# Shared experts' 704 features in parts of 384 and 320, gate and up of the last 64 in one chunk

## What is computed

```python
xn = layernorm(x)
x = x + attention(xn, Wq, Wk, Wv, Wo) \
      + routed(xn, top2 of 8 experts, 352 features each) \
      + (silu(xn @ sg.T) * (xn @ su.T)) @ sd.T      # shared: sg, su [704, 512], sd [512, 704]
```

## Time and profile before

| | us |
|---|---|
| median of 3 timed runs | 1118.25 (1118.01 to 1118.48) |
| profiled execution | 1127.01 |
| its span, first to last instruction | 1125.0 |
| norm and project phases | 0 to 183 |
| attend phase | 183 to 757 |
| out phase and start of the routed one | 757 to 820 |
| routed phase | 820 to 1125 |
| mean granted TensorE clock | 0.969 |

### The profile page before, as it was taken

The page is one execution under the profiler, slowest core; times in us unless marked ns, Lnnn a source line. Parts: engine busy times, 40 slices in busy tenths (PEclk is TensorE's granted clock), DMA queues, the critical chain, the costliest instruction groups (busy, mean ns, idle before and its releaser), DMA issues. The chain is left out here.

```text
span 1125.0 us, 18890 instructions
## 1 busy us (share of the span) xinstructions
PE 1046.2 (93%) x5379; PEld 817.6 (73%) x5380; DVE 784.6 (70%) x1675; ACT 637.9 (57%) x1278; POOL 506.4 (45%) x568
## 2 busy tenths in 40 slices
PE   6999979888899998999999999998989999999994
PEld 4767867666677776777778777776867777778872
DVE  6732324565688887788888888865568888888872
ACT  3323211265588786787787887872155555565550
POOL 0013903388756564556566565651013443333321
PEclk9999989988899999999999999998989999999997
DMA  6989996255543553644445426118789444443432
GB/s 213 322 335 361 136 293 231 94 67 102 132 133 77 150 148 75 163 118 136 115 113 151 126 64 191 45 39 266 243 283 278 90 76 75 75 72 68 71 54 35
DMA packets 106201, 163.61 MB, mean 145 GB/s; under 512 B 53984, under 2 KB 64480, under 8 KB 102656
## 3 DMA queue, kind: packets, MB, share of 16 engines
q1 hardware_dynamic: 95776, 141.82, 44.1%
q0 software_dynamic: 9760, 20.49, 10.0%
q10 hardware_dynamic: 576, 0.26, 0.1%
HBM read 101.25 MB, written 61.28 MB: 144 GB/s over the span
## 5 line engine op out<-in xcount | busy, mean ns | idle before, releaser
L1198 POOL TENSOR_TENSOR prob_lo<-prob,prob_hi 128x512 fp32r<-128x512 f32 (+2 forms) x320 | 308.3, 977 | 203.3 <-ACT prob_hi L1243 147.0
L1236 ACT ACTIVATE prob<-ps_s 128x512 f32<-128x512 f32 (+3 forms) x384 | 188.0, 490 | 127.1 <-PE ps_s L1463 77.1
L1243 ACT ACTIVATE prob_hi<-prob 128x512 fp32r<-128x512 f32 (+3 forms) x384 | 198.6, 517 | 12.4 <-ACT row_stage L1217 12.4
L1862 DVE TENSOR_TENSOR rw_lo<-gu_sb,rw_hi 128x704 fp32r<-128x704 f32 x156 | 138.8, 893 | 52.7 <-ACT rw_hi L1806 47.7
L1306 DVE CUSTOM_DVE_ANT_0 ps_m<-ps_m,causal 128x384 f32<-128x384 f32 (+3 forms) x256 | 126.7, 495 | 69.2 <-PE ps_m L1432 66.9
L1806 ACT ACTIVATE rw_hi<-gu_sb 128x704 fp32r x156 | 123.5, 794 | 62.8 <-PE ps_ru L1895 43.6
L1458 PE MATMUL ps_s<-qs,ks 97*128 97x512 f32 (+3 forms) x384 | 140.4, 366 | 9.4 <-ACT prob L1236 9.2
L1779 POOL DMA_INDIRECT out<-work,slot_table x39 | 63.5, 1627 | 181.1 <-DVE work L1847 148.2
L1481 PE MATMUL ps_o<-prob_hi,vs 128*66 128x512 f32 (+3 forms) x384 | 133.1, 347 | 10.4 <-issue 9.6
L1432 PE MATMUL ps_m<-ks,qs 96*128 96x512 f32 (+3 forms) x384 | 139.1, 362 | 0.6 <-DVE maxima L1306 0.2
L1483 PE MATMUL ps_o<-prob_lo,vs 128*66 128x512 f32 (+3 forms) x384 | 132.0, 344 | 0.0
(11 more groups left out here) (201 smaller groups left out, 2353.0 us busy)
## 6 DMA issues: line engine op xcount, KB each, us to landing
xt<-xt_blocks SPq DMA_DIRECT2D x7, 2048.0 KB, 9.1
v_rows<-work SPq DMA_DIRECT2D x16, 512.0 KB, 3.0
xt_blocks<-xt SPq DMA_DIRECT2D x4, 2048.0 KB, 11.3
qk_hi<-work SPq DMA_DIRECT2D x8, 1024.0 KB, 4.7
qk_lo<-work SPq DMA_DIRECT2D x8, 1024.0 KB, 7.5
qs<-qk_hi SPq DMA_DIRECT2D x64, 128.0 KB, 2.9
ks<-qk_hi SPq DMA_DIRECT2D x64, 128.0 KB, 3.2
vs<-v_rows SPq DMA_DIRECT2D x32, 256.0 KB, 4.7
```

What stands on the lines that cost most here:

```text
L1198: nc.gpsimd.tensor_tensor(prob_lo[:, s % NPL, 0:w], prob[:, s % NP, 0:w], prob_hi[:, s % NPH, 0:w].bitcast(F32), ALU.subtract).then_inc(lo ...
L1236: nc.scalar.activation(prob[:, s % NP, 0:w], ps_s[s % NS][:, 0:w], ACT.Exp, scale=SCALE).then_inc(exp_done, 1)
L1243: nc.scalar.activation(prob_hi[:, s % NPH, 0:w], prob[:, s % NP, 0:w], ACT.Copy).then_inc(hi_ready, 1)
L1862: nc.vector.tensor_tensor(w_lo[:, k, :], chunk(e, k), w_hi[:, k, :].bitcast(F32), ALU.subtract).then_inc(w_lo_ready, 1)
```

## The change

The parts become 384 and 320 features: SHARED is three chunks of 128 for part 0, and 128, 128 and 64 for part 1. The last chunk of part 1 is mixed: its 64 gate and 64 up features are laid side by side in sg, one group of 12 matmuls computes both, gates in partitions 0 to 63 and ups in 64 to 127 of one bank. A unit of part 1 then has 96 matmuls instead of 108. Since the group count of these units is odd, BANK says which bank a unit begins with. Tanh, gate and hidden follow each other on the one bank; hidden and its two successors of a mixed chunk are put one step later. The first two y-adds are brought forward where the bank's next use would come in an earlier step. Gate, up and down weights of the shared experts are laid out over all 704 features in HBM, and part 0 is loaded in three DMAs instead of four. slot and pick now share the memory of started.

```diff
 FCH = [(0, 128), (128, 128), (256, 96)]
+FSH = NSH * F
+SHARED = [[(0, 128), (128, 128), (256, 128)], [(0, 128), (128, 128), (256, 64)]]
+PART_AT = [0, 3 * P]
+def is_mixed(part, k):
+    return SHARED[part][k][1] < P
...
-    UP_END = [2 * GROUP * (k + 1) for k in range(NF)]
-    PER_UNIT = UP_END[-1] + 4 * 3 * NF
+    GATE_END, UP_END = [], []
+    for part in range(2):
+        ends = [0]
+        for k in range(NF):
+            ends += [ends[-1] + GROUP, ends[-1] + (1 if is_mixed(part, k) else 2) * GROUP]
+        GATE_END.append(ends[1::2])
+        UP_END.append(ends[2::2])
+    PER_UNIT = [up_end[-1] + 4 * 3 * NF for up_end in UP_END]
+    BANK = [sum(is_mixed(n // NTB, NF - 1) for n in range(unit)) % 2 for unit in range(UNITS)]
...
-    TANH_AT, GATE_AT = chunks_at(GROUP, 1), chunks_at(GROUP, 2)
-    HIDDEN_AT, HIDDEN_HI_AT, HIDDEN_LO_AT = [chunks_at(2 * GROUP, lag) for lag in (1, 2, 3)]
+    TANH_AT, GATE_AT = [chunks_at(GATE_END, lag, lag) for lag in (1, 2)]
+    HIDDEN_AT, HIDDEN_HI_AT, HIDDEN_LO_AT = [chunks_at(UP_END, lag, lag + 1) for lag in (1, 2, 3)]
...
-        ADD_AT.setdefault(step_of(n // 4, Y_END[n % 4] - 1) + 1, []).append(n)
+        unit, q = divmod(n, 4)
+        end = Y_END[unit // NTB][q]
+        taken = step_of(unit, end + (3, 9)[q]) if q < 2 else ALL
+        ADD_AT.setdefault(min(step_of(unit, end - 1) + 1, taken), []).append(n)
...
-    SPLIT_AT = {step_of(LAST, UP_END[k] - 1) + 2: [k] for k in range(NF)}
+    SPLIT_AT = {step_of(LAST, UP_END[0][k] - 1) + 2: [k] for k in range(NF)}
...
+        def second_places(k, gates, ups):
+            f0, w = SHARED[1][k]
+            if is_mixed(1, k):
+                return (gates, slice(f0, f0 + w)), (gates, slice(f0 + w, f0 + 2 * w))
+            return (gates, slice(f0, f0 + w)), (ups, slice(f0, f0 + w))
...
-                    f0, w = FCH[k]
+                    f0, w = SHARED[1][k]
                     wait(sp, gu_lo_ready, 2 * k)
                     for n, src in enumerate((sgate, sup)):
-                        sp.dma_start(gu_raw[:, n, :, 0:w], src[1, :, :, f0:f0 + w]
+                        at = PART_AT[1] + f0
+                        sp.dma_start(gu_raw[:, n, :, 0:w], src[:, :, at:at + w]
...
+                        up_of = ps_f[bank][w:2 * w, :] if mixed(n) else ps_f[1 - bank][0:w, :]
+                        nc.vector.scalar_tensor_tensor(hid[0:w, :], gated[0:w, :], 0.5, up_of,
+                                                       ALU.mult, ALU.mult).then_inc(hid_ready, 1)
...
-                    last = nc.tensor.matmul(ps_f[part][0:w, :],
-                                            (w_hi, w_lo, w_hi)[term][:, kc, f0:f0 + w],
+                    last = nc.tensor.matmul(ps_f[(BANK[unit] + part) % 2][:, :],
+                                            (w_hi, w_lo, w_hi)[term][:, kc, f0:f0 + P],
...
-                        if q < 2:
-                            pe.wait_ge((gated_ready, hid_ready)[q], NF * (unit + 1))
+                        if q >= 2:
+                            pe.wait_ge(y_added, 4 * unit + q - 1)
+                        elif mixed(chunks - 1):
+                            pe.wait_ge(hid_ready, chunks - 1 + q)
                         else:
-                            pe.wait_ge(y_added, 4 * unit + q - 1)
+                            pe.wait_ge((gated_ready, hid_ready)[q], chunks)
...
-                pool.wait_ge(shared_loaded, 64)
-                w = FCH[-1][1]
-                for n, (raw, (hi, lo)) in enumerate(zip((sg_raw, su_raw), shared_w)):
+                pool.wait_ge(shared_loaded, 48)
+                for n, (raw, (hi, lo)) in enumerate(zip((sg_raw, su_raw, sd_raw), shared_w)):
```

More of the change, by code:

```diff
@@ L43 @@
 FCH = [(0, 128), (128, 128), (256, 96)]
+FSH = NSH * F
+SHARED = [[(0, 128), (128, 128), (256, 128)], [(0, 128), (128, 128), (256, 64)]]
+PART_AT = [0, 3 * P]
+assert PART_AT[1] + sum(w for _, w in SHARED[1]) == FSH
+def is_mixed(part, k):
+    return SHARED[part][k][1] < P
 NORM_SLOTS, YS = 4, 4
@@ L843, in step_cost, with chunks_at @@
         return cost
-    FILL = fill_counts([step_cost(s) for s in range(ALL)], UNITS * PER_UNIT, 0, STEPS + AHEAD, 228.0)
+    FILL = fill_counts([step_cost(s) for s in range(ALL)], BEGIN[-1], 0, STEPS + AHEAD, 228.0)
     FILLED = [sum(FILL[:s]) for s in range(ALL + 1)]
     def step_of(unit, m):
-        return next(s for s in range(ALL) if FILLED[s + 1] > PER_UNIT * unit + m)
-    def chunks_at(after, lag):
+        return next(s for s in range(ALL) if FILLED[s + 1] > BEGIN[unit] + m)
+    def chunks_at(ends, lag, lag_mixed):
@@ L854, in chunks_at @@
         found = {}
         for n in range(UNITS * NF):
-            found.setdefault(step_of(n // NF, 2 * GROUP * (n % NF) + after - 1) + lag, []).append(n)
-        return found
-    TANH_AT, GATE_AT = chunks_at(GROUP, 1), chunks_at(GROUP, 2)
-    HIDDEN_AT, HIDDEN_HI_AT, HIDDEN_LO_AT = [chunks_at(2 * GROUP, lag) for lag in (1, 2, 3)]
+            unit, k = divmod(n, NF)
+            found.setdefault(step_of(unit, ends[unit // NTB][k] - 1)
+                             + (lag_mixed if mixed(n) else lag), []).append(n)
@@ L912, in attend_phase @@
         started = sbuf("started", [P, NST, E])
-        slot = sbuf("slot", [P, NT, E])
-        pick = sbuf("pick", [P, NT, E])
+        slot, pick = [started[:, n * NT:(n + 1) * NT, :] for n in range(2)]
         before = sbuf("before", [P, NT, E])
@@ L992, in load_xt @@
                 def load_xt(unit):
-                    wait(sp, up_done, NF * unit)
+                    wait(sp, gate_done, NF * unit)
+                    wait(sp, up_done, ups(NF * unit))
                     sp.dma_start(xt[:, :, :, :].bitcast(F32), xt_dram[unit % NTB]
@@ L1507, in gate_or_up @@
                         if unit == LAST + 1:
-                            pe.wait_ge(gu_lo_ready, 2 * k + part + 1)
+                            pe.wait_ge(gu_lo_ready, 2 * k + (2 if mixed(n) else part + 1))
                         if k:
-                            pe.wait_ge((gated_ready, hid_ready)[part], NF * unit + k)
+                            pe.wait_ge((gated_ready, hid_ready)[part], n)
                         else:
```

112 lines of the change are left out of this document (55 added, 57 removed).

## The result

The changed kernel takes 1127.01 us (median of 5 runs, 1126.41 to 1128.89) against 1118.01 us for the kernel before (median of 5 by then, 1113.33 to 1118.48): a ratio of 1.0095, 95% interval 1.0072 to 1.0118. On a second chip the ratio was 1.0076 (1.0050 to 1.0103). The prediction was 1115.4 us, and the time lies outside its range. The change makes the kernel 0.8 to 0.9% slower (9.0 and 7.4 us by the medians).

The account below looks back on a forecast made before the run. The prediction took TensorE's own instruction list to bound the kernel from 302 to 757 us. Its terms, -11.2 + 0.9 + 0.8 + 3.4 + 2.2 + 1.0 + 1.1 - 1.0 = -2.8, gave 1115.4 us, range 1109.5 to 1121.0.

Parts of the forecast that it names:

- (a): Shared experts on TensorE: 48 gate and up matmuls removed at 0.233 us each, 11.2 us less work.
- (b): Part of the saving off the path: 0.9 us in GpSimd's stretch, 0.8 us where ScalarE or VectorE is next.
- (f): Waits between the shared experts' own steps, mixed chunk's chain and y-sums: +1.1 us together, between -2 and +4.
- (c): Second gate and up weight piece: two steps instead of four from release to split, ScalarE and TensorE wait; cost 3.4 us.
- (d): Third weight piece, queued behind the slot table's load at head 16, arrives later and pauses TensorE; cost 2.2 us.
- (e): TensorE's granted clock at 0.50 for longer after the two lengthened pauses; cost 1.0 us together.
- (g): Unit 4's token block, loaded at head 17 without the slot table, no longer comes late: -1.0 us.
- (h): Projection phase: GpSimd's wider splits and SyncE's larger loads are hidden by GpSimd's 40.7 us wait; no cost.
- The base: Profiled execution of the kernel before, 8.8 us above the timed median; the prediction took all of it as common.
- The slower case: Third piece behind the slot table blocks and lands late, with longer half-clock stretches: +2.9 us, 1121.1 us; chance 0.20.
- The stalls eat it all: VectorE or ScalarE holds TensorE up in many steps: -0.5 us, 1117.8 us, no change; chance 0.25.

Follow-up runs that it names:

- both: Changed kernel, third-chunk down matmuls of part 1 over 128 zero-padded rows, splits 2, 6, 8 steps after their chunks: 1115.45 us, 0.9926 of the kernel before.
- plain_both: The kernel both with the 48 matmuls put back (no mixed chunk), splits 2, 6, 7 steps after their chunks: 1114.31 us, 0.9914 of the kernel before.
- tiny_lo: The kernel both with VectorE's six lower-part subtractions covering 8 of 512 columns: 1110.92 us, 0.9890 of the kernel before.
- both2: The kernel both repeated unchanged on another chip: 1113.17 us, 0.9916 of the kernel before.
- again: The kernel before, unchanged, profiled once more on another chip: 1123.62 us (span 1121.7), beside a median of 1122.39 there.
- rows128: Changed kernel with part 1's third-chunk down matmuls reading 128 rows, 64 of them zero weights: 1121.70 us, 0.9988 of the kernel before.
- k64_plain: Changed kernel with the mixed chunk off: all 864 matmuls, plan of before, 64-row down matmuls kept: 1130.66 us, 1.0069 of the kernel before.

## Why the prediction was wrong

The prediction had the change 2.8 us faster, and it is 9.0 and 7.4 us slower by the medians. The step that failed is (a): it put the down matmuls of the third chunk, which go from 96 rows to 64, at nothing, and they cost 7.3 us. The second is what (b) and (f) set aside for waits on VectorE (0.8 and 1.1 us): the split stage and the last stage lost 8.8 us in that way, only in part explained.

Stage by stage, mean of the two executions before against the mean of the two after: -3.4, -2.1, +4.7, -0.9, +6.9, together +5.2 us. By cause:

```
48 matmuls less, at 0.233                                            -11.2
64-row down matmuls (239.4 - 232.1)                                   +7.3
late weight pieces, now 10.3, before 8.8                              +1.5
split stage else: first split moved in, VectorE late (3.3 + 0.9)      +4.2
last stage else: 22 matmuls (5.1) gave 0.5                            +4.6
steps 24 to 156: 15 matmuls (3.5) gave 2.1                            +1.4
steps 0 to 24: 3 matmuls (0.7) gave 3.4                               -2.7
sum                                                                   +5.1
```

The 3.3 is 51.8 (both) less 48.5 (plain_both). Of the 4.2 us, 2.7 are the two waits beside the first split, and tiny_lo gave 2.9 back; the rest is not shown. With both2's 54.5 in place of 51.8, the third line would be -1.2 and the fourth +6.9; their sum doesn't depend on it.

Point by point, by the prediction's letters.

- **(a), the step that failed first.** "A matmul's length is its 512 columns in both" was said of the gate and up matmuls and true of them. The down matmuls of the third chunk went from 96 rows to 64 in the same edit, and no step of the sum priced that; +7.3 us. The row count stands in the diff (256, 96 becomes 256, 64), and the 0.233 itself was right: stage 192 to 228 lost 4 matmuls and 0.9 us.
- **(b), an engine next in line, priced 0.8 us.** The reasoning (a cut of 27 ns a step against 12 us of idle time) took the engines as evenly loaded and the surroundings of each event as unchanged. They are not: the first split moved to a place beside four of GpSimd's subtractions, where VectorE's part takes 3.37 us and not 1.63. The split stage lost 4.2 us beyond the late pieces, and the prediction had 2.5 as the upper end. The 0.9 us set aside for GpSimd's stretch did come, and as much again: steps 36 to 72 take 71.6 us in both executions before and 72.6 and 72.5 after, though 4 matmuls are gone from them.
- **(c), (d), (e), the late pieces: mechanism right, size too large.** The waits came (4.03 and 4.23 us, expected 4.5 to 5.5 and more), as did the 3.56 us issue in the third piece's way and the lower clock. But the pauses of TensorE were 3.46 and 3.77 us, not 5 to 6, and before's own, with what followed, had already cost 8.8 us. Net +1.5 where the three letters had 6.6. In (d) the restart by its own terms is +13.0 (11.3 + 1.7) and not +12.8, a slip of 0.2 us.
- **(f), the chains.** The wait for hid in unit 4 was forecast at 2.0 us and was 1.85; the waits for y_acc were 1.6 us, with 2.7 forecast. Unit 0's waits (hid, hid_lo, y_acc: 0.9, 1.4 and 1.2 us) shrank to 0.3, 0.9 and 0.5, more than the 0.5 us expected, which with 3 matmuls (0.7) makes 2.5 of the 3.4 us that steps 0 to 24 gained. But the mixed chunk in last place costs 3.2 us in the last stage against first place, and all the last stage's 4.6 us were lost where +1.1 net had been put down. What the 1.4 us beyond the mixed chunk's place are is open; most of the loss lies in steps 228 to 300, which take 95.2 us in both and 93.6 in plain_both, though 10 of the 22 matmuls are gone from there.
- **(g)** held: no wait for xt in unit 4 after. It had been 1.0 and, in the second execution, 2.6.
- **(h)** held. GpSimd's wait at the end of the projection phase is shorter (40.7 in the earlier trace rows) and still covers all:

```profile
POOL causal L1214 <- POOLq L507: 36.9, 1, 36.9
```

- **The base.** The difference of 8.8 us between the profiled execution and the timed ones belonged to that execution: again's lay 1.2 us above the median of its chip, and the kernel after was profiled at 1128.24 us, 1.2 above its median. Against its own trace the prediction (1124.2) missed by 4.0 us, against the median by 11.6. What of the 9.0 us between the medians lies outside the 5.2 that the stages show is not found: the part before the first maximum was in fact shorter in the traces after (181.6 and 176.9, against 184.3 and 180.3).
- **The rivals.** The slower case (1121.1) had its place right, the third piece behind the slot table, and was the nearest; its price came about through something else, so its nearness is luck. "The stalls eat it all" through VectorE, a quarter, is the other half of what happened. Neither had a term for the rows.

Not tried: moving the down matmuls of 64 rows next to each other, which would make fewer changes of rows; the fewer matmuls with the first split kept away from GpSimd's run; and freeing VectorE at the splits by giving the subtractions to another engine.

## What to carry to other kernels

Price an edit by every shape it changes, not only by the instructions it removes: here the time saved at 48 matmuls was lost for two thirds at 48 others, whose operands had lost a third of their rows. Where an engine is 97% busy, what it waits for once it is faster can't be read from mean loads; look in the trace for the places where the next engine was only just in time, and for what an event will stand beside once the plan has moved it. Compare stages at the same granted clock. And take the profile's base from several executions: here one of them lay 8.8 us off.

## What the runs showed of the hardware

- A change between 64 rows and more cost TensorE 0.15 us on the mean of 48 changes (after against rows128) and 0.14 us on that of 62 (k64_plain against before); between 96, 97 and 128 rows nothing was seen. Padding with zero rows to 96 was as good as to 128.
- VectorE's subtraction of 512 fp32 elements per partition with both inputs in SBUF took 0.68 us, and 1.62 to 1.78 us when it fell beside GpSimd's subtractions of the same size (both). One of 8 elements took 1.10 us there, the five after it 0.15 or 0.16 us (tiny_lo).
- The same wait of TensorE for VectorE, 2.2 us, was followed by a granted clock of 1.00 in one execution and 0.50 in another (both, both2), which made the stage 2.7 us longer.
- The issue behind the slot table's load blocked SyncE's queue for 3.55 and 4.13 us in the two executions before and 3.56 and 3.24 us in the two after, and for 3.18 to 3.56 us in the other thirteen, whichever load it was (xt in the plan of before, vs in the other); so it goes with the place behind the slot table and not with the load that is issued.
